# One gelu block per pair of row tiles in a differential-attention layer with a ternary feed-forward

## The reference, cut to what matters

```
x = x + attention(layernorm(x))          # x: 8 batches x 1024 rows x 512
x = x + ffn(layernorm(x))

attention: q = x Wq.T (32 heads of 16), k = x Wk.T (16 of 16, each used twice), v = x Wv.T
           rotary embedding on q and k; scores = q k.T / 4, causal; softmax
           diff = probs[even head] - lambda * probs[odd head]
           out  = rms_norm(diff @ v) * subln_weight * (1 - lambda_init), then @ Wo.T
ffn:       w1_q, w2_q = ternary(w1), ternary(w2)     # -1, 0, 1 by 0.7 * mean|w|
           h   = gelu(x @ w1_q.T + b1)               # exact gelu; 2048 features
           out = h @ w2_q.T + b2
```

## Time and profile before

| | |
|---|---|
| time, median of 3 runs (lowest to highest) | 4144.07 us (4143.53 to 4144.22) |
| the profiled execution, its own time | 4135.7 us |
| its span, first to last instruction | 4133.9 us |
| mean granted TensorE clock | 0.949 of full |
| PE busy | 3484.3 us (84%) |
| DVE busy | 3184.0 us (77%) |
| ACT busy | 2895.2 us (70%) |
| POOL busy | 1759.8 us (43%) |
| one batch in the loop | about 504 us |

### The profile page before, as it was taken

One profiled execution on the slowest core, in us unless ns is written; L12 is line 12 of the kernel. 1 busy time (PEld: TensorE's weight loads), 2 busy tenths in 40 slices (PEclk: granted clock), 3 DMA queues, 4 the chain that ended last, 5 costly groups with the idle time before them and its releaser, 6 DMA issues.

```text
span 4133.9 us, 84084 instructions
## 1 busy us (share of the span) xinstructions
PE 3484.3 (84%) x23454; PEld 2098.3 (51%) x23454; DVE 3184.0 (77%) x5185; ACT 2895.2 (70%) x6798; POOL 1759.8 (43%) x2322
## 2 busy tenths in 40 slices
PE   4788988888888888888888888888888888888888
PEld 2455555455455554555555545555555455455555
DVE  6878877788677886788767887777877788777784
ACT  4577766788667876677766777667776677667774
POOL 1145433454334533345433544335443444434444
PEclk7899999999999999999999999999999999999999
DMA  4000011100101011000011010110001010010000
GB/s 149 29 29 21 20 34 34 34 15 30 35 24 34 18 32 35 30 24 29 21 34 34 20 34 16 34 34 26 28 19 39 27 34 20 30 34 23 32 20 22
DMA packets 146888, 128.57 MB, mean 31 GB/s; under 512 B 66656, under 2 KB 117728, under 8 KB 145888
## 3 DMA queue, kind: packets, MB, share of 16 engines
q1 hardware_dynamic: 146400, 122.79, 9.1%
HBM read 67.61 MB, written 55.12 MB: 30 GB/s over the span
## 4 chain that ended last, share of the span: by engine, by line
PE 43%; DVE 21%; issue 19%; ACT 12%; POOL 2%; DMA 1%; ACTq 1%; SPq 1%; DVEq 1%; POOLq 0%
PE M L958 9%; PE F L1030 7%; DVE NM L769 7%; PE SP_ L973 6%; PE M L1008 6%; PE F L1047 5%; PE DP L985 4%; DVE NM L777 4%; DVE E L796 3%; ACT E L619 3%; ACT DT L631 2%; PE M L952 2%; ACT L619 2%; ACT L636 2%; PE DX L985 1%
## 5 line engine op out<-in xcount | busy, mean ns | idle before, releaser
L619 ACT ACTIVATE E<-SP_,NM 128x256 f32<-128x256 f32 (+7 forms) x2048 | 1522.5, 744 | 945.6 <-DVE NM L777 546.2
L769 DVE TENSOR_REDUCE NM<-SP_ 128x1 f32<-128x896 f32 (+3 forms) x1024 | 1031.8, 1018 | 285.8 <-PE SP_ L974 282.3
L973 PE MATMUL SP_<-KST,QST 96*128 96x512 f16 (+3 forms) x3072 | 829.3, 341 | 365.3 <-ACT E L619 317.2
L796 DVE SCALAR_TENSOR_TENSOR E<-E,CC 128x512 f32<-128x512 f32 (+7 forms) x1024 | 940.5, 919 | 50.7 <-POOL CC L527 31.4
L985 PE MATMUL DP<-ident,E 128*128 128x128 f32 x3328 | 573.0, 287 | 99.2 <-DVE E L796 89.0
L973 PEld LDWEIGHTS SP_<-KST,QST 96*128 96x128 f16 x3072 | 274.2, 101 | 707.9 <-ACT E L619 490.2
L631 ACT ACTIVATE DT<-DP 128x512 f32<-128x512 f32 (+3 forms) x1024 | 525.1, 513 | 112.1 <-PE DP L985 104.6
L524 POOL TENSOR_TENSOR RP<-SUM,minus 128x1 f32<-128x1 f32 x512 | 290.8, 568 | 723.3 <-ACT E L619 710.6
L777 DVE TENSOR_REDUCE NM<-SP_ 128x2 f32<-128x1024 f32 (+3 forms) x512 | 419.1, 819 | 190.4 <-PE SP_ L974 187.1
L958 PE MATMUL M<-WQKV,WT 128*128 128x512 f32 x1040 | 543.4, 616 | 16.0 <-DVE TOK L870 8.0
L985 PEld LDWEIGHTS DP<-ident,E 128*128 128x128 f32 x3328 | 387.4, 147 | 262.3 <-issue 141.5
(11 more groups left out here) (123 smaller groups left out, 4903.8 us busy)
## 6 DMA issues: line engine op xcount, KB each, us to landing
scratch<-SPL SPq DMA_DIRECT2D x65, 576.0 KB, 2.7
QST<-scratch SPq DMA_DIRECT2D x390, 64.0 KB, 2.4
X<-in_x SPq DMA_DIRECT2D x66, 256.0 KB, 2.7
out<-SQ SPq DMA_DIRECT2D x63, 256.0 KB, 2.1
KST<-scratch SPq DMA_DIRECT2D x390, 32.0 KB, 1.9
DT<-in_w1T SPq DMA_DIRECT2D x2, 1024.0 KB, 12.8
DT<-in_w2T SPq DMA_DIRECT2D x2, 1024.0 KB, 8.8
WQKV<-in_wqT SPq DMA_DIRECT2D x1, 1024.0 KB, 6.5
```

What stands on the lines that cost most here:

```text
L619: act.activation(dst, score_out(i, 2 * n + k, w), ACT.Exp, bias=NM[:, (2 * u + k) % 8:(2 * u + k) % 8 + 1], scale=1.0, accum_out=SUM[:, i ...
L769: nc.vector.tensor_reduce(NM[:, m:m + 1], score_out(i, 2 * n + k, P * (i + 1)), AX.X, ALU.max, negate=True).then_inc(max_ready, 1)
L796: nc.vector.scalar_tensor_tensor(out=E1[:, u % 4, 0:w], in0=E2[:, u % 2, 0:w], scalar=CC[:, u % 4:u % 4 + 1], in1=E1[:, u % 4, 0:w], op0=A ...
L973: pe.matmul(SP_[:, k[a // 512], 0:n], q, KST[0:ROWS, a // P:(a + n) // P, kk, :], start=True, stop=not last)
```

## The change

Both gelu instructions of a pair run at half step 0 of the even tile, one right behind the other. `HP` now holds all 16 feature tiles. `HL` has no memory of its own any more: it is a view of `HP`, and each low part overwrites the front half of its own float32 row. All eight splits of a pair are in the even tile, at half steps 3, 5, 7, 8, 9, 11, 13 and 15. The second product has no lump: for the first row tile it runs over half steps 9 to 19 and for the second over 21 to 30, all 16 feature tiles each, and the first waits for each split at the step that needs it. The first output addition moves from half step 17 to 20. ACT's wait for the splits before L680 is gone, since nothing is overwritten. Two temporary uses of `HP` and `HL` in the setup follow the new layout.

```
-GELU_ODD, GELU_EVEN = 14, 0
-SPLIT_ODD, SPLIT_EVEN = (16, 18, 20, 22), (2, 4, 6, 8)
+GELU_AT = 0
+SPLIT_AT = (3, 5, 7, 8, 9, 11, 13, 15)
-W2_LUMP, W2_REST, W2_NEXT = 1, (10, 7), (18, 13)
-OUT_AT = (17, 31)
+W2_AT = ((9, 11), (21, 10))
+OUT_AT = (20, 31)
...
-        if hs == W2_LUMP:
-            return 0, range(0, GELU_F)
-        for j, f0, (at, n) in ((0, GELU_F, W2_REST), (1, 0, W2_NEXT)):
+        for j, (at, n) in enumerate(W2_AT):
             if at <= hs < at + n:
-                return j, range(f0 + (FT - f0) * (hs - at) // n, f0 + (FT - f0) * (hs - at + 1) // n)
+                return j, range(FT * (hs - at) // n, FT * (hs - at + 1) // n)
...
-        HP = sb("HP", [P, GELU_F, 2 * P], F32)
+        HP = sb("HP", [P, FT, 2 * P], F32)
-        HL = sb("HL", [P, FT, 2 * P], F16)
+        HL = HP[:, :, :].rearrange("p a b -> p (a b)").bitcast(F16).rearrange("p (a b) -> p a b", a=FT)[:, :, 0:2 * P]
...
-                pool.tensor_tensor(HL[:, fs, :], HP[:, h, :], HH[:, fs, :], ALU.subtract).then_inc(h_ready, 1)
+                pool.tensor_tensor(HL[:, fs, :], HP[:, fs, :], HH[:, fs, :], ALU.subtract).then_inc(h_ready, 1)
...
-                    if T.w1 and hs in SPLIT_ODD:
-                        hidden_split(T.pair, SPLIT_ODD.index(hs))
-                    if T.w2 and hs in SPLIT_EVEN:
-                        hidden_split(T.pair, 4 + SPLIT_EVEN.index(hs))
+                    if T.w2 and hs in SPLIT_AT:
+                        hidden_split(T.pair, SPLIT_AT.index(hs))
...
-            def gelu(q, j):
-                after(act, hp_ready, 8 * q + 4 * j + 4)
-                act.activation(HP[:, :, :], HP[:, :, :], ACT.Gelu).then_inc(gelu_done, 1)
+            def gelu(q):
+                after(act, hp_ready, 8 * q + 8)
+                for j in range(0, FT, GELU_F):
+                    act.activation(HP[:, j:j + GELU_F, :], HP[:, j:j + GELU_F, :], ACT.Gelu).then_inc(gelu_done, 1)
...
-                        after(act, h_ready, n - 3)
...
-                    if T.w1 and hs == GELU_ODD:
-                        gelu(T.pair, 0)
-                    if T.w2 and hs == GELU_EVEN:
-                        gelu(T.pair, 1)
+                    if T.w2 and hs == GELU_AT:
+                        gelu(T.pair)
...
                 if fs[0] == 0:
-                    hold(pe, h_ready, 8 * q + 4)
                     hold(pe, hp_ready, 8 * q + 8)
                     hold(pe, o_sum, 2 * q + j)
+                if j == 0:
+                    hold(pe, h_ready, 8 * q + fs[-1] // 2 + 1)
                 for f in fs:
-                    if f == GELU_F and j == 0:
-                        hold(pe, h_ready, 8 * q + 8)
```

More of the change, by code:

```diff
@@ L366, in diff_attention_ffn @@
         w2f = [draw[:, 2 * FF:3 * FF], draw[:, 3 * FF:4 * FF], HH[:, :, :].rearrange("p a b -> p (a b)").bitcast(F32),
-               HL[:, :, :].rearrange("p a b -> p (a b)").bitcast(F32)]
+               HP[:, GELU_F:FT, :].rearrange("p a b -> p (a b)")]
         raw = (w1f, w2f)
         cut = [q[:, :, :].rearrange("p a b -> p (a b)") for q in (W1Q, W2Q)]
-        low = HP[:, :, :].rearrange("p a b -> p (a b)").bitcast(BF16).rearrange("p (a b) -> p a b", a=2)
+        low = HP[:, 0:GELU_F, :].rearrange("p a b -> p (a b)").bitcast(BF16).rearrange("p (a b) -> p a b", a=2)
         def hold(eng, signal, value):
@@ L391, in end_rows @@
         def end_rows(k):
-            return slice(2 * k % GELU_F, 2 * k % GELU_F + 2), slice(2 * k, 2 * k + 2)
+            return slice(2 * k, 2 * k + 2)
         block = ctx.enter_context(nc.Block())
@@ L511, in hidden_split @@
                 hold(pool, f2_ready, 2 * q)
-                pool.tensor_scalar(HH[:, fs, :], HP[:, h, :], 1.0, 0.0, ALU.mult, ALU.add).then_inc(h_chain, 1)
+                pool.tensor_scalar(HH[:, fs, :], HP[:, fs, :], 1.0, 0.0, ALU.mult, ALU.add).then_inc(h_chain, 1)
                 after(pool, h_chain, n + 1)
-                pool.tensor_tensor(HL[:, fs, :], HP[:, h, :], HH[:, fs, :], ALU.subtract).then_inc(h_ready, 1)
+                pool.tensor_tensor(HL[:, fs, :], HP[:, fs, :], HH[:, fs, :], ALU.subtract).then_inc(h_ready, 1)
             def ratio(b, i, n):
@@ L580, in _ @@
             for k in range(1, FT // 2, 2):
-                h, fs = end_rows(k)
+                fs = end_rows(k)
                 pool.wait_ge(end_gelu, k + 1)
                 hold(pool, f2_ready, 2 * LAST)
-                pool.tensor_scalar(HH[:, fs, :], HP[:, h, :], 1.0, 0.0, ALU.mult, ALU.add).then_inc(end_high[1], 1)
+                pool.tensor_scalar(HH[:, fs, :], HP[:, fs, :], 1.0, 0.0, ALU.mult, ALU.add).then_inc(end_high[1], 1)
                 pool.wait_ge(end_high[1], k // 2 + 1)
-                pool.tensor_tensor(HL[:, fs, :], HP[:, h, :], HH[:, fs, :], ALU.subtract).then_inc(end_split[1], 1)
+                pool.tensor_tensor(HL[:, fs, :], HP[:, fs, :], HH[:, fs, :], ALU.subtract).then_inc(end_split[1], 1)
         @block.scalar
@@ L677, in act_work @@
                         after(act, f1_ready, n + 1)
-                        after(act, h_ready, n - 3)
                         for f in (2 * k, 2 * k + 1):
-                            ins = act.activation(HP[:, f % GELU_F, :], F[:, 2 * P * (f % 2):2 * P * (f % 2) + 2 * P],
+                            ins = act.activation(HP[:, f, :], F[:, 2 * P * (f % 2):2 * P * (f % 2) + 2 * P],
                                                  ACT.Identity, bias=b1c[:, f:f + 1], scale=1.0 / XS)
                         ins.then_inc(hp_ready, 1)
-                    if T.w1 and hs == GELU_ODD:
-                        gelu(T.pair, 0)
-                    if T.w2 and hs == GELU_EVEN:
-                        gelu(T.pair, 1)
+                    if T.w2 and hs == GELU_AT:
+                        gelu(T.pair)
             def abs_chunk(j, k):
@@ L692, in abs_chunk @@
                 hold(act, abs_part, 4 * j + k)
-                act.activation(HP[:, :, :].rearrange("p a b -> p (a b)"), raw[j][k], ACT.Abs,
+                act.activation(HP[:, 0:GELU_F, :].rearrange("p a b -> p (a b)"), raw[j][k], ACT.Abs,
                                accum_out=wsum[:, j, k:k + 1]).then_inc(abs_part, 1)
@@ L703, in _ @@
             every_block(act, act_work)
-            act.wait_ge(h_ready, 8 * LAST)
+            act.wait_ge(f2_ready, 2 * LAST)
             for k in range(FT // 2):
-                h, fs = end_rows(k)
+                fs = end_rows(k)
                 act.wait_ge(end_f1, k + 1)
-                if k >= 4:
-                    act.wait_ge(end_split[k % 2], (k - 4) // 2 + 1)
                 for j in range(2):
-                    ins = act.activation(HP[:, h.start + j, :], SP_[:, k % 4, 2 * P * j:2 * P * j + 2 * P], ACT.Gelu,
+                    ins = act.activation(HP[:, fs.start + j, :], SP_[:, k % 4, 2 * P * j:2 * P * j + 2 * P], ACT.Gelu,
                                          bias=b1c[:, fs.start + j:fs.start + j + 1], scale=1.0 / XS)
@@ L932, in _ @@
             for k in range(0, FT // 2, 2):
-                h, fs = end_rows(k)
+                fs = end_rows(k)
                 dve.wait_ge(end_gelu, k + 1)
                 dve.wait_ge(f2_ready, 2 * LAST)
-                nc.vector.tensor_copy(HH[:, fs, :], HP[:, h, :]).then_inc(end_high[0], 1)
+                nc.vector.tensor_copy(HH[:, fs, :], HP[:, fs, :]).then_inc(end_high[0], 1)
                 dve.wait_ge(end_high[0], k // 2 + 1)
-                nc.vector.tensor_tensor(HL[:, fs, :], HP[:, h, :], HH[:, fs, :], ALU.subtract).then_inc(end_split[0], 1)
+                nc.vector.tensor_tensor(HL[:, fs, :], HP[:, fs, :], HH[:, fs, :], ALU.subtract).then_inc(end_split[0], 1)
             dve.wait_ge(end_res, 2)
```

1 line of the change is left out of this document (removed).

## The result

| | before | changed |
|---|---|---|
| median of 4 runs (lowest to highest) | 4144.15 us (4143.53 to 4144.72) | 4208.56 us (4204.35 to 4210.48) |
| ratio, 95% interval | | 1.0165 (1.0153 to 1.0177) |
| span of the profiled execution | 4133.9 us | 4202.5 us |

The change makes the kernel slower, by 64 us in the median and 68.6 us in the two profiled spans. The forecast of 4255 us had the sign and the places, and 46 us too much.

A forecast was written before the change was run, and what follows sets the result against it. PE was taken to bound the greater part of an even block, from half step 8 on. Terms -112 + 60 + 58 + 37 + 61 + 7 = +111 on 4135.7 gave 4247, plus 8.4 to the median 4255 us; range 4180 to 4325.

The forecast's parts named there:

- odd hole and its slow clock: In half steps 14 to 18 of odd blocks, PE's idle and slow-clock time comes back: -112 us, from -90 to -145.
- splits leaving the odd block: Four splits leave the odd block's POOL, for whose ratio DVE waits 31.4 us: a few us, within the -112.
- second gelu at half step 0: In even blocks it costs 1.91 plus 0.02 us and nothing takes this up: +60 us, 45 if some is absorbed.
- half steps 1 to 7 of even blocks: After PE idles about 6.4 us at half step 0, a half clock slows attention: +37 us, bounds 0 and 75.
- moved matmuls: In even half steps 9 to 30, 1.0 of 3.45 us vanishes: 74 us, less 16 hidden behind POOL, +58.
- POOL late in blocks 4 and 6: In half steps 8 to 15, ratios stand behind four more splits and DVE waits: +61 us, bounds 0 and 95.
- closing: In the first closing block, eight splits, square, power and scaling stand ahead of PE's last rows: +7 us.
- second rival: In blocks 4 and 6 POOL is in time, so 61 us go and 16 come back: 4210 us, chance 0.20.
- first rival: ACT sets the pace, PE has room, only 62 table loads count, 79.5 us saved: 4064 us, chance 0.12.
- The fourth: Over the whole kernel the parts cancel, odd gain -145 and POOL 0: +33, or no change at 4144; chance 0.05.
- The third, dearer: POOL, slow clock and matmuls at their bounds, odd gain 100: +228; with two at bounds about +185, 4330 us; chance 0.13.

The follow-up runs named there:

- no odd gelu: The kernel before with the odd block's gelu replaced by an identity on 128 columns that needs no table load, splits kept: 4034.76 us, ratio 0.9751.
- only the matmuls moved: The kernel before with only the second product placed as in the changed kernel, half steps 9 to 19 and 21 to 30, no lump: 4207.10 us, ratio 1.0168.

## Why the prediction was right, and where its sizes were off

All terms are for the whole kernel; a batch's figure times 31/4 pairs.

| term | predicted | measured | by |
|---|---|---|---|
| odd hole and its slow clock | -112 | -102 | 13.2 per batch, no odd gelu |
| splits leaving the odd block | within the above | -22 | the rest of 16.0 per batch |
| second gelu at half step 0 | +60 | +56 | 7.2 per batch |
| half steps 1 to 7 of even blocks | +37 | +22 | 2.9 per batch |
| moved matmuls | +58 | +44 | 5.7 per batch, only the matmuls moved |
| POOL late in blocks 4 and 6 | +61 | +65 | 8.4 per batch, against only the matmuls moved |
| closing | +7 | +8 | 70.4 and 78.1 us |
| sum | +111 | about +70 | the spans differ by 68.6 |

The direction was right, and each step that the prediction named is in the trace; the sizes were off, and one term was counted twice. What bounds the even block, a PE that is full from half step 8 on, is what made the cover worth more than the two table loads. Removing 62 loads took 79 us from ACT. What left the odd blocks, a gelu with a load on each side, gained 102 there, since PE ran out of scores under it and had a slow clock behind it; it was lost again in the even ones.

The mis-sized terms are four. First, the four splits that left the odd block: the prediction called them worth a few microseconds by DVE's wait of 31.4 us, and they gave 22. A wait was the wrong place to look: of the 1.2 us by which blocks 5 and 7 each differ, with and without their splits, about 1.1 are DVE's busy time. No run has the splits alone moved out of the odd block, so this is read from two traces and not from an experiment of its own. The rest of the term, hole and slow clock, was put at the upper end for a like reason: the clock in the earlier trace rows is that of one batch, 13.7 us at half speed, and the same half steps have 8.5 in the mean of batches 2 to 7. Second, the moved matmuls: of 3.45 us per pair the prediction let 1.0 vanish in PE's idle time and 2.0 did (5.7 per batch are 1.4 per pair). The prediction held that idle time at certain steps isn't room that moved work finds. It mostly was: with only the matmuls moved, PE's idle time in half steps 8 to 30 of an even block falls from 2.7 to 1.1 us in the mean of batches 2 to 7. Third, the slow clock: 22 us were measured in half steps 1 to 7 where 37 were predicted, and 14 of them went when PE was kept at work. It was put down to the hole of over 6 us; the run with only the matmuls moved has it as well, with a hole of 4.5 us. Fourth, the second gelu: its 1.93 us stand in full in half step 0, +56, but taking most of it out gave 31 us where 46 were due, so by itself it is worth about 40.

The term counted twice is the 16 us taken off the moved matmuls because they hide behind POOL. POOL's lateness of 5.7 and 4.0 us was already worked out against PE's pace with the moved matmuls in it. Like for like the matmuls were put at 74 us, against 44 measured, and without the slip the forecast would have been 4271.

The POOL step was the best sized, +61 against +65, both against a kernel with the matmuls moved. It held by its steps too: in half steps 8 to 15 POOL's busy time was to be 20.8 and 20.1 us and is 18.33 and 19.03, and the stretch is 5.4 and 4.3 us longer than with only the matmuls moved, where 5.7 and 4.0 were said before a microsecond was taken off. Blocks 4 and 6 grew by 8.6 and 7.2 us (8 to 9 was said), 0 and 2 by 4.7 and 3.4 (5 to 6 was said), and the wait for CC rose from 31.4 to 81.7 us. The second rival, "POOL is in time", gave 4210 us, which is the time that was measured. It is refuted all the same: POOL was late and cost its 65 us, and the other terms together came out some 44 us below the forecast. A time that fits is no proof of the mechanism that predicted it.

The first rival, ACT sets the pace and PE has room, would have given 4064 us. It fell with the run in which only the matmuls move, which it put at 4144 to 4152 and which took 4207. The fourth, that the parts cancel, is out for this kernel. With the splits placed so that hardly a ratio is late they do cancel, at 1.0009, by smaller terms on both sides than that rival had. The third, dearer, stayed far off, and none of its bounds was reached.

## What to carry to other kernels

Before two pauses of an engine are merged into one, look at what another engine does during each: here one pause was nearly free because it had 3.45 us of matmuls under it, which also kept the clock up, and the merged one had nothing. Work on a third, half idle engine must be placed against the deadlines of what stands behind it in its own list; the same eight splits cost 66 us more at one set of half steps than at another, and a placement that repays only part of the debt shows almost no gain.

## What the runs showed of the hardware

With a piece of the first product in the odd hole and the next at half step 20, the granted clock fell to 0.72 in block 1 although the longest single wait of PE in the 8 us before it was 1.2 us; PE was busy 1.31 of the 2.70 us just ahead. In the kernel before, the same block had one wait of 1.83 us in the hole, PE busy 4.15 of 5.80 us, and the clock stayed at full in it and behind it, as the two windows from half step 14 on show. So idle time spread over several short waits can cost the clock where one longer wait did not. The waits ahead don't settle it alone: with the next piece at half step 18 they are the same (1.2 us at the longest, PE busy 1.27 of 2.60 us in the fifth batch), and the clock stayed at full in five of six batches. No run shows what the chip goes by.

```profile
1620.50:1626.30 5.80, 4.15 (x22) 2.26 (x20) 2.63 (x8) 5.74 (x8) 1.82 (x4) 1.00 0.00 0
1628.20:1634.20 6.00, 5.46 (x56) 3.93 (x53) 5.07 (x13) 5.36 (x19) 4.87 (x6) 1.00 0.02 4
```

DVE was busy longer where POOL split beside it: with the splits in block 5 its 72 instructions took 55.24 us, and 54.25 without them. And POOL's own second split instruction takes 1254 ns in the mean in the changed kernel and 1337 with two splits at half step 1, where the kernel is 66 us faster; so an instruction's own time says little about what its place costs.
